# Attention on one core: when the products with V are issued in TensorE's order

## The reference

```python
x = x + tanh(g_xattn[0]) * xattn(layernorm(x), ctx_768, ...)   # 4 x 1024 queries, 4 x 2048 keys
x = x + tanh(g_ffn[0]) * ffn(layernorm(x), ...)
# in xattn, 16 heads of D = 32:
attn = softmax(clip(q @ k.T * D ** -0.5, -10000, 10000))       # per head 1024 x 2048
out  = attn @ v                                                # per head 1024 x 32
```

## Time and profile before

| | us |
|---|---|
| median of 3 runs | 3110.64 |
| lowest, highest run | 3108.18, 3110.97 |
| the profiled execution | 3112.01 |
| its span, first to last instruction | 3110.2 |
| PE, DVE, ACT, POOL busy | 2996.1, 2119.5, 1709.5, 1837.2 |
| mean granted clock of PE | 0.98 of full speed |

### The profile page before, as it was taken

How to read it: one execution, slowest core, us unless ns; L and a number is a source line. 1 busy time by engine, 2 the same in 40 slices (tenths; PEclk the granted TensorE clock), 3 DMA queues, 4 the chain that set the end, 5 groups by cost and what they waited for, 6 DMA issues and landing times. The chain is left out here.

```text
span 3110.2 us, 51282 instructions
## 1 busy us (share of the span) xinstructions
PE 2996.1 (96%) x15462; PEld 1807.1 (58%) x15462; DVE 2119.5 (68%) x3020; ACT 1709.5 (55%) x3096; POOL 1837.2 (59%) x887
## 2 busy tenths in 40 slices
PE   8999979999999999999999999999969799999999
PEld 6888854444444444444444444444426577777777
DVE  5555557676676767667676666767647787777775
ACT  3222227776766767767776767767732344444443
POOL 4655548888888888888888888888844000000000
PEclk9999989999999999999999999999989799999999
DMA  6667742222212222221221222122159200000000
GB/s 203 226 220 237 226 173 62 54 49 61 60 42 61 61 49 53 61 59 43 61 61 46 56 61 56 46 61 60 24 148 292 109 28 28 18 25 26 21 21 28
DMA packets 139855, 254.72 MB, mean 82 GB/s; under 512 B 16946, under 2 KB 57970, under 8 KB 132596
## 3 DMA queue, kind: packets, MB, share of 16 engines
q1 hardware_dynamic: 139764, 253.60, 28.9%
HBM read 162.32 MB, written 91.23 MB: 82 GB/s over the span
## 5 line engine op out<-in xcount | busy, mean ns | idle before, releaser
L836 DVE TENSOR_REDUCE at_half_max<-ps 128x1 f32<-128x1024 f32 x1024 | 1208.7, 1220 | 542.0 <-PE ps L654 534.9
L583 POOL TENSOR_TENSOR at_gp_sum<-at_gp_sum,at_probT 128x1024 f32<-128x1024 f32 x512 | 1218.2, 2379 | 42.3
L778 ACT ACTIVATE at_probT<-ps 128x512 f32<-128x512 f32 x2048 | 1060.0, 603 | 226.5 <-PE ps L673 226.5
L654 PE MATMUL ps<-k_stack,q_stack 96*128 96x512 f32 x2048 | 701.6, 424 | 15.8 <-issue 12.1
L673 PE MATMUL ps<-q_stack,k_stack 98*128 98x512 f32 x2048 | 659.8, 403 | 1.6 <-ACT at_probT L778 1.3
L654 PEld LDWEIGHTS ps<-k_stack,q_stack 96*128 96x128 f32 x2048 | 345.0, 191 | 397.0 <-issue 222.5
L712 PE MATMUL ps<-at_probT,v_head 128*32 128x512 f32 x4096 | 492.5, 598 | 0.9 <-ACT at_probT L778 0.9
L673 PEld LDWEIGHTS ps<-q_stack,k_stack 98*128 98x128 f32 x2048 | 385.9, 189 | 171.2 <-ACT at_probT L778 99.3
L578 POOL TENSOR_TENSOR at_gp_sum<-at_probT 128x1024 f32<-128x1024 f32 x128 | 305.2, 2384 | 298.1 <-ACT at_probT L778 298.1
L1383 POOL TENSOR_TENSOR x_keep<-x_keep,b_half 128x2048 f32<-128x2048 f32 x8 | 37.5, 4682 | 550.4 <-DVE x_keep L1406 550.4
L1436 DVE SCALAR_TENSOR_TENSOR ff_acc<-ps,s_t,ff_acc 128x512 f32<-128x512 f32 x384 | 288.0, 750 | 20.3 <-PE ps L1312 0.4
(11 more groups left out here) (172 smaller groups left out, 3638.8 us busy)
## 6 DMA issues: line engine op xcount, KB each, us to landing
k_stack<-kT_hi SPq DMA_DIRECT2D x128, 256.0 KB, 5.0
kT_hi<-pi_out_hi SPq DMA_DIRECT2D x16, 1024.0 KB, 4.4
kT_lo<-pi_out_lo SPq DMA_DIRECT2D x16, 1024.0 KB, 6.7
v_heads<-pi_v_out SPq DMA_DIRECT2D x16, 1024.0 KB, 10.4
q_stack<-qT_hi SPq DMA_DIRECT2D x128, 128.0 KB, 3.4
k_stack<-kT_lo SPq DMA_DIRECT2D x64, 256.0 KB, 4.3
v_head<-v_heads SPq DMA_DIRECT2D x64, 256.0 KB, 5.1
pi_c_in<-in_ctx_dram SPq DMA_DIRECT2D x16, 768.0 KB, 9.9
```

Source lines behind the costliest of these rows:

```text
L583: pool.tensor_tensor(gp_sum[lane % 2][:, :, :], gp_sum[lane % 2][:, :, :], pairs[:, 2 * i + 2:2 * i + 4, :], ALU.add).then_inc(gp_added, 1)
L654: mm = pe.matmul(ps[:, n, :], q_stack[buf][0:PARTS, rows], k_stack[buf][0:PARTS, BANK * n:BANK * (n + 1)], start=True, stop=True)
L778: act.activation(probT[lane % 2][:, kv, :], src, ACT.Exp).then_inc(exp_done, 1)
L836: dve.tensor_reduce(dst, src, AX_X, ALU.max).then_inc(max_done, 1)
```

## The change

The lags of the two `values` calls are 9 and 10 before, and 10 and 10 after. In step A PE issues no product with V; in step B it issues all four rounds, one after the other, where it issued two. The waits, the instructions and the data are the same. ACT's copy of the partial values hangs on the second lag (L794), which stays.

```diff
-    TURN, KEYS, PV, SUMS, FOLD = 5, 6, (9, 10), 11, 12
+    TURN, KEYS, PV, SUMS, FOLD = 5, 6, (10, 10), 11, 12
```

## The result

The changed kernel is slower: 3138.62 us (median of 4 runs, 3135.63 to 3139.07) against 3110.45 us (4 runs). The ratio is 1.0091 with a 95% interval of 1.0078 to 1.0104, so +28 us, between 24 and 32. The forecast was the same sign and 3130 us, +19; the range ended at 3138.0, just short of the measured time.

The account below looks back on a forecast made before the run. The prediction took PE's sequence as the bound, 14.35 us a unit: 0.18 at the turn and 0.29 at key tile 1 against 0.31 saved, taken as 0.15 for 128 units, +19 us, 3130 us; range 3092 to 3138.

Parts of the forecast that it names:

- the chain: ACT between the turn and key tile 1: exponentials 12 and 13, copy L790, exponential 14; key tile 1 0.29 us late.
- Merging the blocks saves switching: On PE, one narrow block in place of two: 0.03 + 0.11 + 0.12 + 0.05 = 0.31 us saved a unit.
- turn behind key tile 13: PE, step A: the turn waits for tile 11's exponential and starts at 1216.70 in place of 1216.52, 0.18 us later.
- from the turn to key tile 1: PE: 1.93 us unhindered; waiting for tile 14's exponential, key tile 1 starts at 1218.92 in place of 1218.63.
- The high end of the unknown: ACT around copy L790: no overlap on either side, next exponential 0.61 us after the copy's start, PE at 1218.92.
- the term at the entry of the block: PE, step B: the block of narrow products follows key tile 1 after 0.35 us, its wait falling away.
- the walk: Step-by-step timing of one unit from key tile 13 to the next scores: 0.16 us longer a unit, taken as 0.15.
- One of the signs: On PE at key tile 1: some 35 us of L673 waiting for L778, where it was 1.3.
- Overlap everywhere: Rival: ACT's instructions overlap on both sides of copy L790, key tile 1 unhindered; -17 us, 3094 us; chance 0.18.
- overlap ahead of the copy only: Rival: on ACT, L790 overlaps the exponential before it, not the one behind; 3108 us; chance 0.19.
- A long block running slower: Rival: PE's narrow block takes 0.45 us a group where 0.43 was counted; 3140 us; chance 0.05.
- ACT is later still: Rival: turn or copy 0.1 us later, delaying every later key tile in the ring of three; +0.25 a unit, 3143 us; chance 0.08.

Follow-up runs that it names:

- overlap_probe: Changed kernel plus eleven unused back-to-back ACT exponentials before the attention, every second on fewer or other partitions; 3139.85 us, though only the spacing was of interest.
- key1_behind: Changed kernel with key tile 1 issued behind the block of four rounds, and ACT's copy of the partial values ahead of exponential 1; 3101.31 us, ratio 0.9970.
- dve_copy: Changed kernel with the turned maxima copied by DVE, between its two maxima of step A, and not by ACT (L790 gone); 3112.18 us, ratio 1.0005.

## Why the prediction was right and where it was wrong

**Right: the sign, the chain and the place.** Merging the blocks saves switching, and the missing block costs more. Step by step, forecast first: turn behind key tile 13, 0.41 and 0.39; copy L790 0.03 after an exponential's end, and so it is; next exponential 0.61 behind the copy, and so it is; from the turn to key tile 1 it is 1218.92 - 1216.70 = 2.22 and 1229.53 - 1227.31 = 2.22; the block of four rounds to the next scores 3.58 and 3.57. The high end of the unknown, chosen from one ACT pair and one DVE instruction, is what the chip does, and overlap_probe shows on what it depends.

**Wrong: the term at the entry of the block.** The prediction let the block follow key tile 1 after 0.35, as where nothing waits. It follows after 1229.95 - 1229.53 = 0.42 (0.428 in the mean over 72 units, against 0.344 before, from key tile 13 to the block in step A). Key tile 1's weight load had waited for ACT and stood bare in front of its product, that is, not hidden under the product before; the profile puts the product's start at the load's start and shows 0.50 for its duration in place of 0.40. So a wait at a weight load costs the wait and, here, another 0.07 to 0.10. That it is the bare load is read from the rows, and no run isolates it; key1_behind speaks for it, where the load of key tile 1 stands behind the block, long after ACT is done, and its product is drawn 0.50 long and holds its successor for 0.34 all the same. The same is at key tile 15, whose load waits at 1228.29: the scores behind it follow 0.33 later and not 0.235, but that lies ahead of key tile 1, which ACT sets anyway. A load that waits stood in a row on which the prediction leaned and which it read for the wait only the earlier trace rows.

In numbers: the walk had +0.16 a unit, taken as 0.15. Over 72 units in the middle of each trace a unit takes 14.36 us before and 14.58 after, +0.22, and all of it lies between key tile 13 and the next scores 2, which are 6.39 and 6.61 apart. Term by term, forecast first: the turn behind key tile 13, 0.41 and 0.37; from there to key tile 1, 2.22 and 2.23; the entry, 0.35 and 0.43; from the block to the next scores, 3.58 and 3.57. The turn is a little early in the mean because one unit in six, in which the loop turns around, has PE late, so that tile 11 is done before the turn comes (0.23 there). The other terms are within 0.02, so the entry alone, 0.08 a unit or 10 us over 128, is the step of the sum that failed; it is about what separates the forecast of +19 us from the measured +28. At the ends of the stage the interval that lost its block (2.9 us) and the block that stands bare behind the last turn (2.2 us) nearly cancel, where the prediction had "under 2".

One of the signs was misread as well. The prediction looked for some 35 us of PE at L673 waiting for L778, in place of 1.3. PE's own wait there is still 1.8 us; the wait is one of the weight load (PEld), and that was 99.3 us before and is 164.1 after.

**The rivals.** Overlap everywhere (0.18) and overlap ahead of the copy only (0.19) are out by the ACT rows of the changed kernel and by the probe. A long block running slower (0.05) is out: 0.429 from group to group in blocks of two rounds, of three and of four alike, though its 3140 us came nearest in the total. "ACT is later still" (0.08, 3143 us) was near as well, but by another mechanism: tile 15 came 1.00 us behind the turn (1228.31 - 1227.31), as in the walk.

By the Trainium skill ("ScalarE: Activation LUTs", section "What ACT_TABLE_LOAD costs") back-to-back ACTIVATEs overlap by about 93 ns, which would have given the first of them. The probe agrees where both start at partition 0 (0.61 to 0.63 long, 0.51 to 0.54 apart) and not where one starts at 64 or 96.

**What the range shows.** It ended 0.6 us short. The forecast's own part (3122 to 3138) held only the spread of terms that I had; a term that every new wait could add was not among them. Its upper end also left out two of the forecast's own rivals, at 3140 and 3143 us, with chances of 0.05 and 0.08.

## What to carry to other kernels

A block of work on a full engine can be the cover under which another engine catches up: before merging or moving it, walk that other engine's chain through the gap and find what its last result releases. Price a new wait at a weight load as the wait and the bare load behind it, and read that from a pair in which the load waited, not from one in which it ran ahead. The whole block need not stay as cover (one round of two was enough here), so split such work unevenly and give each part its own wait. And keep neighbours on ScalarE and VectorE at one start partition where a chain is tight.

## What the hardware showed

- ScalarE overlapped neighbours that both start at partition 0 (0.51 to 0.54 us apart) and not one that starts at 0 and one that starts at 96 or 64 (0.64 or 0.65), at nearly the same duration (0.61 to 0.63). The operation (Identity, copy, exponential) and the number of partitions (2, 96, 128) didn't matter. DVE shows the same: 0.02 to 0.04 us from end to start around its instructions at partition 96, and dve_copy, and an overlap of 0.08 between neighbours that both start at 0 or both at 96.
- The first interval of a narrow block is 0.453 us, later ones 0.429, in blocks of every length here; the interval out of it is 0.54.
- A product whose weight load waited holds up its successor by 0.07 to 0.10 us more (0.428 for 0.344 into a block, 0.331 for 0.235 between full-width products), though the profile draws its start at the load's.
